# A recommender tower on one core: column sums as matmuls of 64 rows by 32 columns in two banks, and units 6 to 19 transposed by VectorE

## The chip, the cores and the metric

The kernel runs on one core of one Trainium2 chip. The metric is the device time of one execution in microseconds (us); three executions of the kernel before are given. The profile shows one execution of it, whose span begins at its first instruction and ends at its last.

## The reference

For 512 examples, 40 embedding rows of 64 numbers are looked up. Each of the 780 pairs of fields gets a bilinear score, and a three-layer network follows:

```python
e = jnp.stack([tbl_0[ids[:, 0]], ..., tbl_39[ids[:, 39]]], axis=1)   # 512 x 40 x 64
viW = jnp.einsum('bpd,pde->bpe', e[:, i_idx], W)                     # W: 780 x 64 x 64
z = jnp.einsum('bpe,bpe->bp', viW, e[:, j_idx])                      # 512 x 780
h = jnp.concatenate([z, dense_ctx], axis=1)                          # 512 x 796
h = jnp.maximum(h @ W_top1 + b_top1, 0.0)                            # 512
h = jnp.maximum(h @ W_top2 + b_top2, 0.0)                            # 256
y = h @ W_top3                                                       # 1
```

All of it is float32.

## The kernel before, in words

Two fields make a unit, so there are 20 units; `x[:, u, :]` holds unit u with its 128 numbers on the partitions and the 512 examples along the row. Units 0 to 3 come from small tables and are picked by matmuls with one-hot rows (L535). Units 4 to 19 are gathered: GpSimd issues eight indirect DMAs for each (L336; 2 fields by 4 chunks of 128 examples), in the order of the units, and they land with the examples on the partitions. So each has to be transposed. Units 4 to 10, 18 and 19 are transposed by TensorE (`transpose_unit`, L587) into the bank `t_ps` (unit 4 into `z_ps`) and copied out by ScalarE (`save_x`, L382). Units 11 to 17 (`FOLDED`) are transposed in squares of 32 by 32 by VectorE (`fold_unit`, L491), after which ScalarE puts the squares in place with 16 small copies (L389). GpSimd's first 24 gathers (units 4, 5 and 6) wait for no product; each later one waits for one product more than the gather before it.

The work on the pairs is cut in 195 **duos** in 49 **rounds** of four (three in the last). For a duo, TensorE multiplies two halves of `x` by weights, as two matmuls of 64 rows by 128 columns that run side by side (`interact`, L611), into one of three slots of `y_ps`. VectorE multiplies that slot by a factor out of `x` into `prod` (L522), the **product** of the duo. Duo d waits until product d - 3 has freed its slot. Two rounds later (`LAG`) TensorE sums `prod` over groups of partitions with a 0/1 matrix `select`: `sum_round` (L632), before the change in matmuls of 128 rows by 32 columns, four side by side, all into the bank `z_ps`. A round has eight of them. From round 25 on GpSimd first adds two products of a round into the other two (L352), and four are left. At every eighth round ScalarE copies `z_ps` out (`save_z`, L418).

A float32 matmul stands in the trace as two MATMUL records, and so does its weight load. A duo is thus 4 records on TensorE, the sums of a round 16 (8 from round 25 on), a transposed unit 4.

The order on each engine is the order in which the code is written: all engines walk the same list of duos. `transposed_at(u)` gives the duo ahead of which unit u is transposed, on TensorE (`transpose_unit`) or on VectorE (`fold_unit`) alike. Every engine works strictly through its own list, so an instruction that waits holds up all that stands behind it. After the last sums come layer 1 (L642), layer 2 (L682) and layer 3 (L691).

Of the kernel before, what the change touches and what calls it, by code (L numbers as in the profile page):

```python
# [12 lines left out]
ROWS = 128  # L13
BANK = 512
FIELDS = 40
DIM = 64
# [19 lines left out]
BLOCK_ROUNDS = QUAD // 4  # L36
# [3 lines left out]
FOLDED = range(11, 18)  # L40
# [24 lines left out]
class Plan:  # L65
# [7 lines left out]
    def __init__(self):  # L73
# [23 lines left out]
        self.blocks = -(-len(self.rounds) // BLOCK_ROUNDS)  # L97


        assert len(self.rounds) == BLOCK_ROUNDS * (self.blocks - 1) + 1 and ROUND * 4 + DENSE == QUAD  # L100
# [68 lines left out]
    def place(self, d, half):  # L169

        r, n = divmod(d, ROUND)
        row = 4 * (r % BLOCK_ROUNDS)
        if not self.is_quad(r):
            row += 2 * (n // 2)
        return r // BLOCK_ROUNDS, 2 * (n % 2) + half, row


def dlrm_tower(nc, ids, hot_ids, lane_rows, tables, w1_in, w2_in, head_in, dense_in, w_in, identity, selector, out):
# [6 lines left out]
    with ExitStack() as ctx:  # L185
# [11 lines left out]
        select = sb("select", [ROWS, 2, 2 * QUAD])  # L197
# [41 lines left out]
        h1_ps = [t_ps[:, :], y_ps[:, 0, 0, :], y_ps[:, 0, 1, :], y_ps[:, 1, 0, :]]  # L239

        h2_ps = [[y_ps[:, 1, 1, :], y_ps[:, 2, 0, :]], h1_ps[0:2]]
        out_ps = y_ps[:, 2, 1, 0:BATCH // 4]
# [113 lines left out]
        def _(act):  # L356
# [75 lines left out]
            if (len(plan.rounds) - LAG) // BLOCK_ROUNDS < NBLK - 1:  # L432
                save_z(NBLK - 2)
# [92 lines left out]
        def _(pe):  # L526
# [88 lines left out]
            def sum_round(r):  # L615

                b, _, row = plan.place(ROUND * r, 0)
                quad = plan.is_quad(r)
                if row == 0 and b:

                    pe.wait_ge(z_saved, b)
                closes = row == QUAD - 4 or r == len(plan.rounds) - 1
# [158 lines left out]
```

## Time and profile before

| | us |
|---|---|
| three executions | 357.65, 359.73, 360.52 (median 359.73) |
| span of the profiled execution | 320.2 |
| TensorE busy in the span | 312.7 |
| VectorE busy | 252.3 |
| GpSimd busy | 237.7 |
| ScalarE busy | 90.3 |

The profiled execution has no time of its own beside its span. Against the median of the three, 39.5 us lie around the span. Busy time counts an engine's overlapping instructions once.

### The profile page before, as it was taken

The page shows a single profiled execution, that of the slowest core. Times are in us where ns is not written, and L with a number is a line of the kernel's source. Part 1 is how long each engine was busy: PE and PEld are TensorE (multiplying, and loading weights), DVE is VectorE, ACT ScalarE, POOL GpSimd, SP SyncE. Part 2 cuts the span into 40 slices and gives each one's busy share as a digit, 9 for nine tenths or more (in the row PEclk, how much of TensorE's full clock was granted, in tenths as well). Part 3 has the DMA queues.
Part 4 walks back from the last instruction along what each step waited for, and adds up shares of the span by engine and source line. Part 5 has one row for each costly group of instructions (what it writes and reads, how often), then busy time and mean ns, then how long its engine had stood idle before and what let it go on. Part 6 is the DMA issues. An engine that isn't in the chain of part 4 may idle for free.

```text
span 320.2 us, 4340 instructions
## 1 busy us (share of the span) xinstructions
PE 312.7 (98%) x1716; PEld 117.5 (37%) x1716; DVE 252.3 (79%) x243; ACT 90.3 (28%) x206; POOL 237.7 (74%) x178
## 2 busy tenths in 40 slices
PE   6899999999999999999999999999999999989996
PEld 2465233332333323333333333333333333323464
DVE  4995987788689888988898899999999999940000
ACT  0203500600106835559976363000000000000032
POOL 3898777777777777776677999999999999940000
PEclk9999999999999999999999999999999999999999
DMA  6981332323323753232323121221121000000000
GB/s 136 358 243 21 82 72 62 92 59 67 87 57 92 253 171 86 61 93 57 88 60 90 41 66 34 66 68 46 52 68 57 0 2 0 0 3 5 12 0 0
DMA packets 14459, 23.27 MB, mean 73 GB/s; under 512 B 3556, under 2 KB 4584, under 8 KB 14312
## 3 DMA queue, kind: packets, MB, share of 16 engines
q1 hardware_dynamic: 7848, 13.96, 15.6%
q0 software_dynamic: 4096, 4.20, 6.4%
q10 hardware_dynamic: 2496, 4.84, 4.5%
q8 instruction: 13, 0.21, 0.3%
q14 instruction: 6, 0.05, 0.0%
HBM read 22.86 MB, written 0.00 MB: 71 GB/s over the span
## 4 chain that ended last, share of the span: by engine, by line
PE 65%; POOL 28%; DMA 3%; DVE 1%; POOLq 1%; ACT 0%; issue 0%; ACTq 0%
PE y_ps L611 33%; POOL prod L352 28%; PE z_ps L632 16%; PE y_ps L642 5%; PE y_ps L535 3%; DMA prod<-in_tbl 2%; PE t_ps L642 2%; PE y_ps L682 2%; PE t_ps L535 2%; PE t_ps L587 1%; DMA prod<-hot_ids 1%; DVE prod L522 1%; POOLq L185 1%; PE t_ps L682 1%; DVE x_quad L463 0%; PE y_ps L691 0%
## 5 line engine op out<-in xcount | busy, mean ns | idle before, releaser
L611 PE MATMUL y_ps<-x,w 64*128 64x512 f32 x780 | 183.3, 605 | 0.2
L336 POOL DMA_INDIRECT gathered<-in_tbl,ids_sb x128 | 130.6, 1020 | 45.7 <-issue 28.5
L522 DVE TENSOR_TENSOR prod<-y_ps,x 128x1024 f32<-128x1024 f32 x89 | 103.2, 1218 | 20.5 <-PE y_ps L611 20.1
L522 DVE TENSOR_TENSOR prod<-y_ps,x_quad 128x1024 f32<-128x1024 f32 x96 | 110.7, 1217 | 4.4 <-PE y_ps L611 3.7
L611 PEld LDWEIGHTS y_ps<-x,w 64*128 64x128 f32 x780 | 70.0, 186 | 108.3 <-issue 79.1
L352 POOL TENSOR_TENSOR prod<-prod 128x1024 f32<-128x1024 f32 x46 | 106.9, 2374 | 0.3
L632 PE MATMUL z_ps<-prod,select 128*32 128x512 f32 x596 | 74.5, 600 | 1.3 <-POOL prod L352 1.3
L389 ACT COPY x<-x_fold 32x128 f32<-32x128 f32 x112 | 33.1, 296 | 18.1 <-DVE x_fold L491 16.9
L632 PEld LDWEIGHTS z_ps<-prod,select 128*32 128x32 f32 x596 | 14.4, 108 | 54.1 <-issue 37.6
L418 ACT COPY zT<-z_ps 128x512 f32<-128x512 f32 x6 | 3.5, 586 | 100.6 <-PE z_ps L632 100.6
L412 ACT COPY x_mix<-x 64x512 f32<-64x512 f32 x40 | 24.7, 617 | 0.7
L382 ACT COPY x<-t_ps 128x512 f32<-128x512 f32 x8 | 4.7, 586 | 54.1 <-PE t_ps L587 54.1
L642 PE MATMUL y_ps<-zT,w 128*128 128x512 f32 (+1 forms) x42 | 17.0, 604 | 0.0
L399 ACT COPY x_quad<-x 32x512 f32<-32x512 f32 x24 | 14.8, 616 | 0.4
L522 DVE TENSOR_TENSOR prod<-y_ps,x_mix 128x1024 f32<-128x1024 f32 x10 | 11.8, 1217 | 1.9 <-issue 1.9
L642 PEld LDWEIGHTS y_ps<-zT,w 128*128 128x128 f32 (+1 forms) x42 | 7.0, 189 | 9.2 <-issue 9.2
L456 DVE TENSOR_SCALAR prod<-prod,lane_rows_sb 128x1024 bf16<-128x1024 int16 x16 | 6.9, 490 | 3.6 <-DMA lane_rows_sb<-lane_rows 3.2
L535 PE MATMUL y_ps<-prod 128*64 128x512 bf16 x32 | 6.7, 443 | 1.4 <-DVE x_quad L463 1.1
L642 PE MATMUL t_ps<-zT,w 128*128 128x512 f32 (+1 forms) x14 | 6.5, 606 | 0.0
L456 DVE TENSOR_SCALAR x<-prod,lane_rows_sb 128x1024 bf16<-128x1024 int16 x16 | 6.5, 477 | 0.0
L535 PE MATMUL y_ps<-prod,x_quad 128*64 128x512 bf16 x32 | 5.9, 381 | 0.6 <-DVE prod L456 0.6
L587 PEld LDWEIGHTS t_ps<-ident,gathered 128*128 128x128 f32 x32 | 3.4, 141 | 6.2 <-issue 6.2
(46 smaller groups left out, 87.5 us busy)
## 6 DMA issues: line engine op xcount, KB each, us to landing
w<-w_rows SPq DMA_DIRECT2D x48, 256.0 KB, 2.7
gathered<-in_tbl,ids_sb POOLq DMA_INDIRECT x128, 2.5
w<-w_rows ACTq DMA_DIRECT2D x1, 1792.0 KB, 8.0
prod<-in_tbl ACTq DMA_DIRECT2D x6, 256.0 KB, 8.5
prod<-hot_ids SPq DMA_DIRECT2D x4, 256.0 KB, 6.7
prod<-in_tbl ACTq DMA_DIRECT2D x4, 128.0 KB, 3.1
w<-w_rows ACTq DMA_DIRECT2D x1, 512.0 KB, 9.7
w<-w_rows SPq DMA_DIRECT2D x1, 192.0 KB, 2.3
```

Of the source, the lines that this page charges most:

```text
L336: nc.gpsimd.indirect_dma_start(gathered[:, slot, c, s * DIM:(s + 1) * DIM], None, tables[f][:, :], bass.IndirectOffsetOnAxis(ap=ids_sb[:, ...
L352: nc.gpsimd.tensor_tensor(prod[:, low, :, :], prod[:, low, :, :], prod[:, high, :, :], ALU.add).then_inc(added, 1)
L389: last = nc.scalar.copy(to[:, :, b * QUAD:(b + 1) * QUAD], x_fold[b * QUAD:(b + 1) * QUAD, u % 2, :, e * QUAD:(e + 1) * QUAD])
L399: last = nc.scalar.copy(x_quad[n * QUAD:(n + 1) * QUAD, u - PAIRED - u % 2 + h, :], x[s * DIM + h * QUAD:s * DIM + (h + 1) * QUAD, u, :])
L412: copied = nc.scalar.copy(x_mix[side * DIM:(side + 1) * DIM, 2 * n + half, :], x[field * DIM:(field + 1) * DIM, unit, :])
L456: nc.vector.tensor_scalar(hot[per_lane * u + q], hot_ids_sb[u], lane_rows_sb[:, q:q + 1], None, ALU.is_equal).then_inc(hot_ready, 1)
L522: nc.vector.tensor_tensor(prod[:, d % PROD_SLOTS, :, :], y_ps[:, d % DUO_SLOTS, :, :], factor, ALU.mult).then_inc(prod_ready, 1)
L535: last = nc.tensor.matmul(hot_ps[u][s * DIM:(s + 1) * DIM, :], weights, hot[per_lane * u + q][:, s * BATCH:(s + 1) * BATCH], start=q == 0 ...
L611: last = nc.tensor.matmul(y_ps[:, d % DUO_SLOTS, half, :], w[rows, r % W_SLOTS, d % ROUND, :], x[rows, units[half], :], start=True, stop=True)
L632: last = nc.tensor.matmul(z_ps[q * QUAD:(q + 1) * QUAD, :], select[:, 1 if quad else 0, QUAD - row:2 * QUAD - row], prod[:, d % PROD_SLOTS ...
L642: done = nc.tensor.matmul(h1_ps[m], w1[rows, b, m * ROWS:(m + 1) * ROWS], zT[rows, b, :], start=first and b == blocks[0], stop=last and b ...
L682: last = nc.tensor.matmul(h2_ps[n][m][:, batch_halves[n]], w2[:, k, m * ROWS:(m + 1) * ROWS], h1[k][:, batch_halves[n]], start=(k == 0), s ...
```

## The change

The sums are made of matmuls of 64 rows by 32 columns, upper and lower rows apart: the upper rows go into `z_ps`, the lower ones into `t_ps`. A round has 16 such matmuls in place of 8, and eight of them have places of their own in the array. A block takes 16 rounds and is then copied out of both banks. The duos' matmuls stay 64 rows by 128 columns. The last round, which has a block of its own, keeps matmuls of 128 rows.

`t_ps` is not free for transposes after the first sums, so only units 4 and 5 are transposed by TensorE, unit 5 ahead of duo 4 where it was ahead of duo 11. `FOLDED` is now units 6 to 19: seven more on VectorE, each with 16 copies of ScalarE in place of one. The rule for the place of a folded unit puts unit 6 ahead of duo 8, unit 7 ahead of duo 16, and so on by eights up to unit 19 ahead of duo 112. Before, units 6 to 10 stood ahead of duos 15, 21, 30, 38 and 46, and units 18 and 19 ahead of 104 and 112. The banks of the three layers are dealt out anew.

```diff
-BLOCK_ROUNDS = QUAD // 4
+BLOCK_ROUNDS = QUAD // 2
...
-FOLDED = range(11, 18)
+FOLDED = range(6, 20)
...
+        if u == HOT_UNITS + 1:
+
+            return ROUND
         if u >= FOLDED.start:
...
-            def save_z(b):
-                act.wait_ge(summed, BLOCK_ROUNDS * (b + 1))
-                nc.scalar.copy(zT[:, b, :], z_ps[:, :]).then_inc(z_saved, 1)
+            def save_z(block):
+                act.wait_ge(summed, BLOCK_ROUNDS * (block + 1))
+                for s in range(2):
+                    nc.scalar.copy(zT[:, 2 * block + s, :], z_halves[s][:, :]).then_inc(z_saved, 1)
...
                 for d in duos:
                     for half in range(2):
-                        _, q, row = plan.place(d, half)
-                        last = nc.tensor.matmul(z_ps[q * QUAD:(q + 1) * QUAD, :],
-                                                select[:, 1 if quad else 0, QUAD - row:2 * QUAD - row],
-                                                prod[:, d % PROD_SLOTS, half, :],
-                                                start=(r % BLOCK_ROUNDS == 0 and d < ROUND * r + 2),
-                                                stop=closes and d >= duos[-1] - 1)
+                        q = 2 * (d % 2) + half
+                        out = slice(q * QUAD, (q + 1) * QUAD)
...
+                        row = 2 * turn + (0 if quad else d % ROUND // 2)
+                        for s in range(2):
+                            rows = slice(s * DIM, (s + 1) * DIM)
+                            last = nc.tensor.matmul(z_halves[s][out, :],
+                                                    select[rows, 1 if quad else 0, QUAD - row:2 * QUAD - row],
+                                                    prod[rows, d % PROD_SLOTS, half, :],
+                                                    start=turn == 0 and d < ROUND * r + 2,
+                                                    stop=turn == BLOCK_ROUNDS - 1 and d >= duos[-1] - 1)
                 last.then_inc(summed, 1)
...
-            layer1(0, full[:-1], first=True)
+
+            pe.wait_ge(prod_ready, ROUND * (len(plan.rounds) - 1) + 1)
+            layer1(0, full[:-2], first=True)
             pe.wait_ge(z_saved, NBLK - 1)
-            layer1(0, full[-1:])
+            layer1(0, full[-2:])
```

VectorE at the start of the duos, before: the first products (5, 2 and 21 of them), with no transpose among the first 46.

```order
L522 TENSOR_TENSOR prod<-y_ps,x 128x1024 x5
L522 TENSOR_TENSOR prod<-y_ps,x_mix 128x1024 x2
L522 TENSOR_TENSOR prod<-y_ps,x 128x1024 x21
L522 TENSOR_TENSOR prod<-y_ps,x_mix 128x1024 x2
L522 TENSOR_TENSOR prod<-y_ps,x 128x1024 x18
L491 STREAM_TRANSPOSE x_fold<-gathered 128x512
```

VectorE at the same place now (L530 is the product, L499 the transpose of a folded unit):

```order
L530 TENSOR_TENSOR prod<-y_ps,x 128x1024 x5
L530 TENSOR_TENSOR prod<-y_ps,x_mix 128x1024 x2
L530 TENSOR_TENSOR prod<-y_ps,x 128x1024
L499 STREAM_TRANSPOSE x_fold<-gathered 128x512
L530 TENSOR_TENSOR prod<-y_ps,x 128x1024 x8
L499 STREAM_TRANSPOSE x_fold<-gathered 128x512
L530 TENSOR_TENSOR prod<-y_ps,x 128x1024 x8
```

The transpose of unit 6 stands behind eight products (duos 0 to 7) and ahead of that of duo 8; that of unit 7 follows eight products later.

TensorE from unit 4 to the second sums, before (two matmuls of L611 are a duo; L587 x4 is a transposed unit):

```order
L587 MATMUL z_ps<-ident,gathered 128x128 x4
L535 MATMUL t_ps<-x,zT 64x512 x16
L611 MATMUL y_ps<-x,w 128x512 x22
L587 MATMUL t_ps<-ident,gathered 128x128 x4
L611 MATMUL y_ps<-x,w 128x512 x2
L632 MATMUL z_ps<-prod,select 32x512 x8
L611 MATMUL y_ps<-x,w 128x512 x6
L587 MATMUL t_ps<-ident,gathered 128x128 x4
L611 MATMUL y_ps<-x,w 128x512 x2
L632 MATMUL z_ps<-prod,select 32x512 x8
```

TensorE at the same place now, down to the first four of the 16 sums of round 0 (L595 is the transpose, L619 the duos, L653 the sums):

```order
L595 MATMUL z_ps<-ident,gathered 128x128 x4
L543 MATMUL t_ps<-x,zT 64x512 x16
L619 MATMUL y_ps<-x,w 128x512 x8
L595 MATMUL t_ps<-ident,gathered 128x128 x4
L619 MATMUL y_ps<-x,w 128x512 x16
L653 MATMUL z_ps<-prod,select 32x512
L653 MATMUL t_ps<-prod,select 32x512
L653 MATMUL z_ps<-prod,select 32x512
L653 MATMUL t_ps<-prod,select 32x512
```

Unit 5's transpose moves from behind 11 duos to behind four, the transposes of units 6 to 10, 18 and 19 are gone from TensorE, and the sums alternate between the two banks.

## Rows read from the trace of the kernel before

**Rows 1.** The page: TensorE's busy time, and the chain that ended last.

```profile
PE 312.7 (98%) x1716; PEld 117.5 (37%) x1716; DVE 252.3 (79%) x243; ACT 90.3 (28%) x206; POOL 237.7 (74%) x178
...
PE 65%; POOL 28%; DMA 3%; DVE 1%; POOLq 1%; ACT 0%; issue 0%; ACTq 0%
```

**Rows 2.** Busy us (count) by stretch: PE, PEld, DVE, ACT, POOL; clock, DMA.

```profile
44.90:175.60 130.70, 130.70 (x764) 45.08 (x760) 110.96 (x99) 62.29 (x160) 96.98 (x103) 1.00 0.35 92
175.60:279.00 103.40, 103.40 (x543) 36.24 (x542) 100.40 (x88) 12.36 (x21) 102.96 (x46) 1.00 0.14 39
```

**Rows 3.** Chain that ended last, rounds of duos: start us, us, what.

```profile
92.01 1.92 PE y_ps L611 x8
93.92 0.59 PE t_ps L587 x4
...
147.68 3.63 PE y_ps L611 x16
151.31 1.85 PE z_ps L632 x16
153.16 3.63 PE y_ps L611 x16
156.80 1.85 PE z_ps L632 x16
...
184.83 0.99 PE z_ps L632 x8
185.82 0.59 PE t_ps L587 x4
```

**Rows 4.** The same chain in the tail: sums between layer 1's matmuls of 128x128.

```profile
285.11 5.35 PE t_ps L642 x12
290.46 1.84 PE z_ps L632 x12
292.30 10.50 PE y_ps L642 x24
```

**Rows 5.** The sums' weight loads: four in the timeline, and the page's mean (ns).

```profile
152.13 0.13 PEld L632 LDWEIGHTS z_ps<-prod,select 128*32 128x32 f32 x4 [0.30 <-issue]
```

```profile
L632 PEld LDWEIGHTS z_ps<-prod,select 128*32 128x32 f32 x596 | 14.4, 108 | 54.1 <-issue 37.6
```

**Rows 6.** Timeline of VectorE: a round's products, then a folded unit.

```profile
148.78 4.62 DVE L522 TENSOR_TENSOR prod<-y_ps,x 128x1024 f32<-128x1024 f32 x4 [0.87 <-PE y_ps L611]
153.32 0.70 DVE L491 STREAM_TRANSPOSE x_fold<-gathered 128x512 f32<-128x512 f32 x1
```

**Rows 7.** Timeline of ScalarE: the copies of one folded unit.

```profile
98.70 4.90 ACT L389 COPY x<-x_fold 32x128 f32<-32x128 f32 x16 [3.56 <-DVE x_fold L491]
```

**Rows 8.** Gathers: POOL busy and count to 44.6 us, the last of them, time to landing.

```profile
0.00:44.60 44.60, 32.38 (x24) 1.00 0.57 157
```

```profile
43.45 0.94 POOL L336 DMA_INDIRECT gathered<-in_tbl,ids_sb  x1 [0.30 <-issue]
```

```profile
DMA to landing us min/median/max: 2.3/2.5/7.5
```

**Rows 9.** Timeline of VectorE (duos 7 to 11) and TensorE (duo 11, round 3).

```profile
39.05 5.74 DVE L522 TENSOR_TENSOR prod<-y_ps,x 128x1024 f32<-128x1024 f32 x5
```

```profile
41.97 1.13 PE L611 MATMUL y_ps<-x,w 64*128 64x512 f32 x4
...
44.88 1.56 PE L611 MATMUL y_ps<-x,w 64*128 64x512 f32 x6
```

**Rows 10.** The same chain: GpSimd's additions.

```profile
191.09 90.58 POOL prod L352 x39
```

**Rows 11.** TensorE: early and later one-hot matmuls; a stretch behind its last matmul (clock 0.71).

```profile
5.39 1.92 PE L535 MATMUL y_ps<-prod 128*64 128x512 bf16 x8 [0.34 <-DMA prod<-in_tbl]
...
28.03 1.92 PE L535 MATMUL t_ps<-x,zT 128*64 128x512 bf16 x16
```

```profile
320.00:323.00 3.00, 0.00 (x0) 0.00 (x0) 0.00 (x0) 0.00 (x0) 0.00 (x0) 0.71 0.03 5
```

More of the change, by code:

```diff
@@ L96, in __init__ @@
         self.duos = [d for r in self.rounds for d in r]
-        self.blocks = -(-len(self.rounds) // BLOCK_ROUNDS)
-        assert len(self.rounds) == BLOCK_ROUNDS * (self.blocks - 1) + 1 and ROUND * 4 + DENSE == QUAD
+        self.turns = len(self.rounds) // BLOCK_ROUNDS
+        self.blocks = 2 * self.turns + 1
+        assert len(self.rounds) == BLOCK_ROUNDS * self.turns + 1 and ROUND * 4 + DENSE == QUAD
         self.gather_after = self.gather_times()
@@ L167, in mixture, with place @@
         }[kind]
-    def place(self, d, half):
+    def place(self, d, half, side):
         r, n = divmod(d, ROUND)
[L172 to L175, printed above, removed]
+        q = 2 * (n % 2) + half
+        if r == len(self.rounds) - 1:
+            return self.blocks - 1, q, 2 * (n // 2) + side
+        block, turn = divmod(r, BLOCK_ROUNDS)
+        if self.is_quad(r):
+            return 2 * block + side // 2, q, 2 * turn + side % 2
+        return 2 * block + side, q, 2 * turn + n // 2
 def dlrm_tower(nc, ids, hot_ids, lane_rows, tables, w1_in, w2_in, head_in, dense_in, w_in, identity, selector, out):
@@ L431, in _ @@
                     save_z((r - LAG) // BLOCK_ROUNDS)
-            if (len(plan.rounds) - LAG) // BLOCK_ROUNDS < NBLK - 1:
-                save_z(NBLK - 2)
+            for block in range((len(plan.rounds) - LAG) // BLOCK_ROUNDS, plan.turns):
+                save_z(block)
             act.wait_ge(summed, len(plan.rounds))
@@ L615, in sum_round @@
             def sum_round(r):
-                b, _, row = plan.place(ROUND * r, 0)
+                block, turn = divmod(r, BLOCK_ROUNDS)
                 quad = plan.is_quad(r)
-                if row == 0 and b:
-                    pe.wait_ge(z_saved, b)
-                closes = row == QUAD - 4 or r == len(plan.rounds) - 1
+                if r == 0:
+                    pe.wait_ge(x_ready, HOT_UNITS + 2)
+                elif turn == 0:
+                    pe.wait_ge(z_saved, 2 * block)
                 if r in plan.added:
@@ L711 @@
     identity = np.eye(ROWS, dtype=np.float32)
-    selector = np.zeros((ROWS, 2, 2 * QUAD), np.float32)
+    selector = np.zeros((ROWS, 3, 2 * QUAD), np.float32)
     for e in range(ROWS):
-        selector[e, 0, QUAD + e // DIM] = 1.0
-        selector[e, 1, QUAD + e // QUAD] = 1.0
+        selector[e, 0, QUAD] = 1.0
+        selector[e, 1, QUAD + e % DIM // QUAD] = 1.0
+        selector[e, 2, QUAD + e // DIM] = 1.0
     W = np.asarray(inputs["L0_rec_W"])
@@ L724 @@
         for half in range(2):
-            b, q, row = plan.place(d, half)
             for side, pair in enumerate(plan.tile_pairs(d, half)):
@@ L730 @@
                 w_rows[half * DIM:(half + 1) * DIM, d, side * n:(side + 1) * n] = (W[p] if i < j else W[p].T)[:, part]
+                b, q, row = plan.place(d, half, side)
                 if b < plan.blocks - 1:
-                    w1_rows[q * QUAD + row + side, b] = W_top1[p]
+                    w1_rows[q * QUAD + row, b] = W_top1[p]
                 else:
                     for m, columns in parts:
-                        w1_rows[m * QUAD + ROUND * q + row + side, b, columns] = W_top1[p, columns]
+                        w1_rows[m * QUAD + ROUND * q + row, b, columns] = W_top1[p, columns]
     pairs = FIELDS * (FIELDS - 1) // 2
```

15 lines of the change are left out of this document (11 added, 4 removed).

## The prediction

> **What bounds the kernel now.** I read the page's chain first [rows 1]: TensorE 65% of the span, GpSimd 28%. TensorE is busy 98% of the time, but that is a mean over stages, so I cut the span [rows 2]. From 44.9 to 175.6 us (rounds 3 to 25) TensorE has no idle time, VectorE has 15%: here every us on TensorE counts and a little more on VectorE costs nothing. From 175.6 to 279 TensorE, VectorE (97%) and GpSimd are all full. GpSimd's additions follow each other every 90.58 / 39 = 2.32 us, 4.65 a round [rows 10]; TensorE's round is 3.63 + 0.99 = 4.62 [rows 3]; VectorE's products come one per 1.12 (five in 5.74, four in 4.62), four in 4.5 [rows 6, 9]. What TensorE saves there is worth nothing. Ahead of 44.9 VectorE sets the pace of the first duos, product behind product [rows 9].
>
> **The sums.** A plain round is 3.63 of duos and 1.85 of sums, 5.48 together, with a folded unit inside it or not: the starts 147.68, 153.16 and 151.31, 156.80 both lie 5.49 apart, and the fold at 153.32 is in the second only [rows 3, 6]. What is in these blocks? In the tail 12 steps of 512 columns take 5.35 and 24 take 10.50 [rows 4], so a step is 5.15 / 12 = 0.429 and a block loses 0.20 on entry. The eight steps of four duos are 3.43, and 3.63 stand there: again 0.20. The sums' 16 records, four at a time, are four steps, 1.72, and 1.85 stand there: 0.13. So the two switches of a round cost 0.33. Afterwards the sums have 32 records, eight at a time: again four steps. The work of the array is the same, and only the 0.33 could shrink. Does it? The two shapes now have the same 64 rows and differ in columns alone. The trace has such a case: the last sums (128x32) stand between layer 1's matmuls (128x128), rows equal, columns not. Their four steps take 1.84, a loss of 0.12, and the block behind them loses 0.20 [rows 4]. That is what switches of rows and columns together cost. I take nothing off.
>
> [...]
>
> There is a small loss instead. Four weight loads of 108 ns each are over in 0.13, so one begins some 7 ns behind the other [rows 5]. With eight places the last begins four times 7 = 0.027 later, and the switch waits for it. In 23 rounds on TensorE's path that is **+0.6**. In the last stage TensorE's round becomes 4.65, level with GpSimd's: **+0.2** for some 20 rounds. Bounds: 0 and 1.2.
>
> **The transposes that leave TensorE.** Units 6 to 10 stand in the middle of a round: 0.59, and the duos are then 1.92 + 1.92 where 3.63 would do [rows 3], 0.80 each. Five make **-4.0**. Unit 18 stands beside a sum block: **-0.6**. Unit 19 (0.59 at 185.82, [rows 3]) lies in the stage in which all three engines are full. Its fold takes 0.70 of VectorE [rows 6], which has 0.1 to spare per round, so 0.6 comes back: **0**. The folds of units 7 to 18 hide in VectorE's 0.87 of idle time per round [rows 6]; if that were gone, 0.7 each.
>
> ScalarE now spends 4.9 us per folded unit where one copy did [rows 7], every second round (11 us). It is under half busy in the pair stage [rows 2]. The tightest unit is 7: folded ahead of duo 16, needed as factor of duo 21, five duos or 6.9 us later, against 0.7 + 4.9. That holds with 1.2 to spare; what is beyond it would be paid once. The copies out of the sums' banks are two in a row now, but only three times, and a whole block of duos (3.6 us) stands ahead of the sums that wait for them. In the tail only banks change hands.
>
> **The gathers.** This is the term that decides. Unit 6 is now folded ahead of duo 8. VectorE's wait for its gathers holds up every later product, and through the three slots TensorE too. Gathers up to unit 6 are 24, and they don't depend on products: GpSimd issues them as fast as it can, one per 1.25 us, and the 24th starts at 43.45 [rows 8]. It lands 2.5 later, say at 46.1 (46.0 to 46.5). The product of duo 8 starts at 39.05 + 1.12 = 40.17 before [rows 9]. So VectorE stands for nearly six us. Before, unit 6 stood ahead of duo 15 and waited for nothing. Step by step: landing 46.1, fold 0.70, product of duo 8 1.25, then wait and weight load some 0.2, and the matmuls of duo 11 start at 48.25. Before they started at 41.97 [rows 9], and from there on both kernels do the same up to round 3. **+6.3.** Unit 5, now ahead of duo 4, meets the same limit (16th gather, ten us earlier, landing near 36), but what it delays is over before 46.1 and costs nothing more. Later units are safe: their gathers come at 10 us per unit, their folds every two rounds, 11 us.
>
> **The sum.** 6.3 - 4.0 - 0.6 + 0 + 0.6 + 0.2 = **+2.5**: a span of 322.7 for 320.2, and with the 39.5 around it 362.2 beside the median of 359.73. Between the bounds of the terms (gathers 6.1 to 6.8, start-up of the sums 0 to 1.2, unit 19 -0.6 to +0.2, unit 7 up to 1) it is 360.8 to 363.8.
>
> **Rivals.** (1) *The clock falls in the hole*, the case on the slower side. Duo 10's matmuls are done near 44.1 (product 7 ends near 42.9, since duo 4 was held to about 37, and one duo takes 1.2), and duo 11's begin at 48.25: over four us without a matmul, where from round 3 on there was no hole at all [rows 2]. [...] At the start the same shape gave 8 records in 1.92 where it later gave 16 [rows 11]: half pace. A fall costs half of the time spent low: at least 1.0 (those 1.92), at most 3.0, if it lasts six us. It decides if the hole is long enough; the time is 363.2 to 365.2, I take 364.3. Against it: no hole of that size inside a trace shows what happens. 0.33.
>
> [...]
>
> (2) *The switches get cheaper after all*, since both shapes split the rows alike. At best the 0.33 goes, but in every second round VectorE with four products and a fold (5.2) caps it at 0.3; the last stage gains nothing. 23 x 0.3 = 6.9, and no 0.6 of staggering: 354.7. For it: no case in the trace has 64 rows on both sides. Against it: the tail's switch. 0.11.
>
> (3) *The change doesn't do what it says*: the eight don't run side by side but four by four. 596 / 8 = 74 groups of two steps would take 0.86 more each, over 420. Against it: two 64-row matmuls already write the same partitions of two banks side by side, and four columns of 128 rows run together. 0.05.
>
> **How the numbers follow.** My forecast has 0.48, the rivals 0.33, 0.11 and 0.05, and 0.03 is left. A measurement of this kernel can tell about 1%, 3.6 us. Faster by more (below 356.1): rival 2, 0.11. Slower by more (above 363.3): rival 3, nearly all of rival 1 and the upper end of the forecast, 0.42. Within: 0.47. The range goes from 357.0, half of rival 2's gain, to 366.5, past rival 1; outside lie rival 3 and most of rival 2.
>
> **What would show it.** VectorE idle for about 5 us ahead of the first transpose of a folded unit, released by a gather, and TensorE idle to 48.2; the granted clock behind it tells rival 1. Round 3 starts 6.3 later, at 51.2. Plain rounds of 5.49 to 5.52, sum blocks of 1.88 or so in four steps, no 0.59 between them. Round 26 starts near 178. Additions every 2.32. If sum blocks are near 1.7 or duo blocks near 3.45, rival 2 holds. I am wrong if the gathers of unit 6 land much before 46, or if the rounds differ from 5.5 by more than 0.1.

## The result, and the profile after

| | median of executions, us | ratio to the kernel before |
|---|---|---|
| before | 358.69 (357.1 to 360.52, 4) | |
| changed | 376.14 (375.49 to 377.02, 4) | 1.057 [1.049, 1.065] |

The medians lie 17.5 us apart, 4.9% of the kernel before. The recorded ratio, 1.057, is taken over fast executions alone, and can't be worked out from the times shown. The prediction was 362.2, and the range of 357.0 to 366.5 doesn't reach the measured time. The profiled execution of the changed kernel has a time of its own: 377.02, with a span of 375.1. So 1.9 us lie around this span, not 39.5. It suggests that the profile of before, with its span of 320.2, came from an execution unlike those that were timed, and e0 below shows it.

The page of the changed kernel, the rows that answer to [rows 1], with the granted clock and two of the costliest groups:

```profile
span 375.1 us, 5562 instructions
...
PE 322.3 (86%) x2272; PEld 116.4 (31%) x2272; DVE 256.7 (68%) x250; ACT 118.9 (32%) x311; POOL 238.6 (64%) x178
...
PEclk9899866999999999999999989999999999999999
...
PE 44%; POOL 36%; DVE 8%; issue 6%; another core or an unknown queue 3%; DMA 2%; POOLq 1%; ACT 0%; ACTq 0%; DVEq 0%
...
L619 PE MATMUL y_ps<-x,w 64*128 64x512 f32 x780 | 193.1, 622 | 42.5 <-DVE prod L530 36.6
L343 POOL DMA_INDIRECT gathered<-in_tbl,ids_sb x128 | 131.5, 1027 | 99.9 <-DVE prod L530 63.8
```

TensorE's share fell from 98% to 86%, GpSimd's from 74% to 64%, VectorE's from 79% to 68%. No engine is full: all of them wait. The windows of the changed kernel, cut at the first duo, round 3, round 26 and round 48 (columns as in [rows 2]):

```profile
30.48:63.56 33.08, 18.34 (x86) 6.34 (x85) 13.96 (x13) 11.41 (x27) 20.97 (x23) 0.74 0.20 47
63.56:230.01 166.45, 135.46 (x1113) 43.62 (x1105) 113.60 (x104) 77.70 (x218) 86.97 (x93) 0.99 0.26 69
230.01:334.00 103.99, 103.78 (x729) 36.18 (x721) 101.86 (x91) 20.40 (x50) 103.71 (x46) 1.00 0.14 40
```

The stage of additions takes 103.99, next to 103.40 in [rows 2]. The pair rounds 3 to 25 take 166.45 where they took some 131, with 135.46 of TensorE's work in them: 31 us are waits. The stretch ahead of round 3 takes 33.08, and it took 15.00 (29.88 to 44.88); its granted clock is 0.74, and in windows of one us it reads 0.50 from 39 to 42 and from 50 to 62 us.

One pair round in the timeline of the changed kernel, VectorE, TensorE's duos, then GpSimd:

```profile
117.85 3.47 DVE L530 TENSOR_TENSOR prod<-y_ps,x 128x1024 f32<-128x1024 f32 x3
123.99 4.62 DVE L530 TENSOR_TENSOR prod<-y_ps,x 128x1024 f32<-128x1024 f32 x4 [2.67 <-PE y_ps L619]
...
117.99 1.13 PE L619 MATMUL y_ps<-x,w 64*128 64x512 f32 x4 [1.48 <-DVE prod L530]
120.93 2.85 PE L619 MATMUL y_ps<-x,w 64*128 64x512 f32 x12
125.27 1.13 PE L619 MATMUL y_ps<-x,w 64*128 64x512 f32 x4 [1.50 <-DVE prod L530]
...
120.70 0.95 POOL L343 DMA_INDIRECT gathered<-in_tbl,ids_sb  x1 [0.30 <-issue]
121.95 0.94 POOL L343 DMA_INDIRECT gathered<-in_tbl,ids_sb  x1 [0.30 <-issue]
125.49 0.94 POOL L343 DMA_INDIRECT gathered<-in_tbl,ids_sb  x1 [2.59 <-DVE prod L530]
```

TensorE begins the first duo of round 11 at 120.93. In [rows 6] VectorE starts its product some 1.2 us behind a round's first matmul (147.61 and 148.78). Here it starts at 123.99, 3.06 behind, and gives TensorE as the reason. But by then TensorE has run all three duos for which there are slots (120.93 + 2.85 = 123.78), and waits in turn for that product. The ring is closed: TensorE waits for VectorE, VectorE for a signal of TensorE, GpSimd for VectorE. Each turn takes 7.28 us.

The semaphores' updates in the trace show where it breaks. The sums of this round end at 121.00, and the signal that they are done arrives at 123.91. The signals of duos 0, 1 and 2, due at 122.06, 122.92 and 123.77, all arrive at 123.97 to 124.09. VectorE's and ScalarE's own signals, those that the trace holds, come within 0.02 us of their instructions' ends. So from 121.00 to 123.91 no signal of TensorE got through, though its matmuls were issued on time; then four came 0.06 apart. In each of the rounds 3 to 21 the sums' signal is 2.8 to 3.2 us late, and it comes 0.95 to 1.12 us behind the end of the last gather of a row of three or four (here 122.90 and 123.91). The ends of matmuls are modelled by the profile, so it can't tell a signal that lags behind its matmul from a matmul that itself ends late; "late signal" stands for both. In the stage of additions, where no gathers run, the sums' signals are 0.08 late.

**One word for what follows.** I call an execution *prompt* if TensorE's signals in the pair rounds come within 0.3 us of the matmuls' ends, and *late* if not. The profile of before is prompt: 0.04 to 0.05 us.

### The profile page after: what moved, and what is told of

Read it like the earlier page. It is cut to its first block, busy times and chain, and to the rows that moved or that the text cites. A ratio compares the mean times of both kernels' runs of the same rounds, so it can differ in the third digit from the quotient of the medians.

```text
span 375.1 us, 5562 instructions
## 1 busy us (share of the span) xinstructions
PE 322.3 (86%) x2272; PEld 116.4 (31%) x2272; DVE 256.7 (68%) x250; ACT 118.9 (32%) x311; POOL 238.6 (64%) x178
## 3 DMA queue, kind: packets, MB, share of 16 engines
q0 software_dynamic: 4096, 4.20, 5.6%
q10 hardware_dynamic: 2496, 4.87, 3.8%
## 4 chain that ended last, share of the span: by engine, by line
PE 44%; POOL 36%; DVE 8%; issue 6%; another core or an unknown queue 3%; DMA 2%; POOLq 1%; ACT 0%; ACTq 0%; DVEq 0%
POOL prod L359 28%; PE y_ps L619 23%; PE z_ps L653 12%; POOL gathered L343 8%; DVE prod L530 8%; PE y_ps L663 6%; PE y_ps L705 2%; DMA ids_sb<-ids_rows 1%; PE t_ps L653 1%; POOLq L191 1%; DMA gathered<-in_tbl,ids_sb 1%; DVE x_fold L499 1%; PE z_ps L646 0%; PE t_ps L714 0%
## 5 line engine op out<-in xcount | busy, mean ns | idle before, releaser
L619 PE MATMUL y_ps<-x,w 64*128 64x512 f32 x780 | 193.1, 622 | 42.5 <-DVE prod L530 36.6
L530 DVE TENSOR_TENSOR prod<-y_ps,x 128x1024 f32<-128x1024 f32 x89 | 103.3, 1218 | 62.9 <-PE y_ps L619 45.8
L619 PEld LDWEIGHTS y_ps<-x,w 64*128 64x128 f32 x780 | 70.5, 189 | 163.0 <-issue 93.1
L530 DVE TENSOR_TENSOR prod<-y_ps,x_quad 128x1024 f32<-128x1024 f32 x96 | 110.7, 1217 | 8.3 <-PE y_ps L619 4.1
L396 ACT COPY x<-x_fold 32x128 f32<-32x128 f32 x224 | 66.2, 295 | 101.6 <-issue 79.3
L653 PE MATMUL z_ps<-prod,select 64*32 64x512 f32 x584 | 75.0, 609 | 1.1 <-POOL prod L359 1.1
L653 PE MATMUL t_ps<-prod,select 64*32 64x512 f32 x584 | 75.0, 609 | 0.0
L653 PEld LDWEIGHTS z_ps<-prod,select 64*32 64x32 f32 x584 | 16.0, 108 | 54.1 <-issue 46.9
L663 PE MATMUL y_ps<-zT,w 128*128 128x512 f32 (+1 forms) x56 | 22.4, 604 | 0.0
L530 DVE TENSOR_TENSOR prod<-y_ps,x_mix 128x1024 f32<-128x1024 f32 x10 | 11.9, 1219 | 6.1 <-issue 5.5
L653 PEld LDWEIGHTS t_ps<-prod,select 64*32 64x32 f32 x584 | 16.0, 108 | 0.0
L499 DVE STREAM_TRANSPOSE x_fold<-gathered 128x512 f32<-128x512 f32 x14 | 9.8, 701 | 0.0
L705 PE MATMUL y_ps<-prod,w 128*128 128x256 f32 x32 | 7.3, 382 | 0.0
L450 ACT ACTIVATE prod<-y_ps,head 128x512 f32<-128x512 f32 x4 | 2.5, 685 | 14.5 <-PE y_ps L663 14.5
```

The costliest lines, as they stand in the source:

```text
L396: last = nc.scalar.copy(to[:, :, b * QUAD:(b + 1) * QUAD], x_fold[b * QUAD:(b + 1) * QUAD, u % 2, :, e * QUAD:(e + 1) * QUAD])
L499: nc.vector.transpose(x_fold[:, u % 2, :, :], gathered[:, u % GATHER_SLOTS, :, :]).then_inc(unit_folded, 1)
L530: nc.vector.tensor_tensor(prod[:, d % PROD_SLOTS, :, :], y_ps[:, d % DUO_SLOTS, :, :], factor, ALU.mult).then_inc(prod_ready, 1)
L619: last = nc.tensor.matmul(y_ps[:, d % DUO_SLOTS, half, :], w[rows, r % W_SLOTS, d % ROUND, :], x[rows, units[half], :], start=True, stop=True)
L653: last = nc.tensor.matmul(z_halves[s][out, :], select[rows, 1 if quad else 0, QUAD - row:2 * QUAD - row], prod[rows, d % PROD_SLOTS, half, :],
L663: done = nc.tensor.matmul(h1_ps[m], w1[rows, b, m * ROWS:(m + 1) * ROWS], zT[rows, b, :], start=first and b == blocks[0], stop=last and b ...
```

## The experiments

**The theories.** A: the profile of before shows an unusual execution, and its usual ones have late signals as well. S: the form of the new sums (64 rows, eight side by side) delays the signals. N: their number does. G: GpSimd's indirect gathers, issued one behind another, hold them back. C, after the second group: whether signals are late at all is a condition of a group of runs, and without it the change costs what its steps add up to.

They ran in six groups, each with executions of the kernel before beside it:

| group | kernel before, us (executions) | kind |
|---|---|---|
| 1: e0 to e3 | 359.18, 354.30 to 364.19 (19) | late |
| 2: e4 to e7 | 322.89, 321.38 to 327.85 (13) | prompt |
| 3: e8 to e10 | 357.75, 354.54 to 359.52 (13) | late |
| 4: e11 to e14 | 324.03, 321.79 to 327.68 (25) | prompt |
| 5: e15, e16 | 324.33, 321.46 to 328.14 (19) | prompt |
| 6: e17 | 323.38, 322.19 to 326.83 (13) | prompt |

No execution of the kernel before lies between 328.2 and 354.2. The kind holds through a group. The chips are numbered, and number 2 stands with group 1 and with group 4, so the number doesn't decide it. The three timings given with the profile (357.65 to 360.52) are of the late kind, the profile is of the prompt kind.

**e0, the kernel before, unaltered.**

> The kernel before, once more, for its spans. The profile shown of it spans 320.2 us, its executions take 357 to 360. Theory A (the profile shown is one fast execution, the usual one is slower inside): the span is near 356 and plain rounds take about 1.4 us more than 5.49. Theory B (39 us lie around the span of this kernel): the span is 320 again, rounds 5.49, sums signalled 0.04 us behind the end of their last matmul.

Measured: 360.75 (356.93 to 362.94, ten executions), ratio 1.0011 [0.9954, 1.0068], span of the profiled one 360.9. The same cuts, and three rounds in its timeline, VectorE and TensorE (L611 duos, L632 sums, L587 a transposed unit):

```profile
30.18:62.70 32.52, 19.48 (x70) 5.85 (x68) 13.67 (x12) 6.69 (x11) 21.39 (x24) 0.74 0.16 40
62.70:216.27 153.57, 136.95 (x765) 44.49 (x761) 111.59 (x100) 62.30 (x160) 86.91 (x93) 0.98 0.27 77
...
109.73 4.62 DVE L522 TENSOR_TENSOR prod<-y_ps,x 128x1024 f32<-128x1024 f32 x4 [0.75 <-issue]
117.41 4.62 DVE L522 TENSOR_TENSOR prod<-y_ps,x 128x1024 f32<-128x1024 f32 x4 [3.05 <-PE y_ps L611]
...
108.56 3.70 PE L611 MATMUL y_ps<-x,w 64*128 64x512 f32 x16
112.19 1.92 PE L632 MATMUL z_ps<-prod,select 128*32 128x512 f32 x16
114.05 1.99 PE L611 MATMUL y_ps<-x,w 64*128 64x512 f32 x8
118.69 1.13 PE L611 MATMUL y_ps<-x,w 64*128 64x512 f32 x4 [1.01 <-DVE prod L522]
```

The kernel before has late signals too, but in every second round only. Of the rounds that begin at 108.56 and 114.05 the first runs through in 5.49, and in the second the product waits 3.05. The sums' signals of the rounds around them are late by 0.05, 3.21, 0.04 and 3.33 us. Two rounds take 13.04 us (108.56 to 121.60), where two of the changed kernel take 14.56. The change meets the lateness twice as often. The 15 us ahead of round 3 are 32.5 in this kernel as well, with a granted clock of 0.74 here too.

**e1, the folds alone.** The kernel before with the two lines that move the transposes:

```diff
-FOLDED = range(11, 18)
+FOLDED = range(6, 20)
...
+        if u == HOT_UNITS + 1:
+            return ROUND
```

> The kernel before with units 6 to 19 folded on VectorE and unit 5 transposed ahead of duo 4; the sums stay 128 rows by 32 columns in one bank. Theory S (the long pair rounds of the changed kernel, 7.28 us, come from the eight-wide sums, whose signal comes 2.9 us behind their last matmul): plain rounds as in the kernel before, the hole ahead of duo 8 and the lower clock stay, time some 12 to 15 us over the same kernel without the hole's loss, about 10 over before. Theory F (they come from the folds and ScalarE's 16 copies): rounds of 7.3 us, time near 376.

Measured: 363.38 (358.09 to 369.28, ten executions), ratio 1.0039 [0.9985, 1.0093]. The pair stage of its trace takes 150.29 us. The larger part of the loss comes from the sums.

**e2, unit 6 folded later.**

```diff
         if u >= FOLDED.start:
+            if u == FOLDED.start:
+                return 12
```

> The changed kernel with unit 6 folded ahead of duo 12, not 8: VectorE has four more products to do until the gathers of unit 6 land. If the hole with its lower clock costs what the profile of the changed kernel shows (round 3 begins at 63.6 us, 18.7 later than before), 8 to 14 us are saved and the clock stays up. If the hole is only moved, 0 to 3 us.

Measured: 376.65, ratio 1.0466 [1.0383, 1.0548], the time of the changed kernel. Round 3 begins at 63.13, where it began at 63.56. So to fold unit 6 later gives next to nothing back; that VectorE stands in this stretch in any case would explain it, but isn't shown apart.

**e3, the sums in another order.** The 16 matmuls of a block: the eight of the upper rows, then the eight of the lower rows. It was meant to have four places in use at a time.

```diff
+                turns = [(d, half, s) for s in range(2) for d in duos for half in range(2)]
```

> The changed kernel with the 16 matmuls of a round's sums in another order: the eight of the upper rows, then the eight of the lower ones. Only four places of the array are then used at a time. If the eight matmuls side by side cause the late signal (theory W, width), the signal comes at most 0.1 us behind the last matmul, the sum block grows from 1.95 to about 3.6 us and rounds of 7.2 us are bound by TensorE. If the number of 64-row matmuls causes it (theory N), the signal is 2.9 us late as before and the round takes 8 us or more.

Measured: 377.34, ratio 1.0486 [1.0407, 1.0564], pair stage 166.0 us as before. But the edit didn't narrow the block. Its first two steps in the timeline, upper rows (`z_ps`) and lower rows (`t_ps`):

```profile
126.47 0.63 PE L646 MATMUL z_ps<-prod,select 64*32 64x512 f32 x4
126.53 0.63 PE L646 MATMUL t_ps<-prod,select 64*32 64x512 f32 x4
126.93 0.61 PE L646 MATMUL z_ps<-prod,select 64*32 64x512 f32 x4
126.98 0.61 PE L646 MATMUL t_ps<-prod,select 64*32 64x512 f32 x4
```

Upper and lower rows still run side by side, and the block takes 1.97 us (126.47 to 128.44) and not the 3.6 that was expected. So the run shows that the order of the sixteen makes no difference. Whether the eight side by side delay the signals it doesn't tell; their number, their 64 rows and their being eight wide all stay possible.

**e4, plain copies for gathers.** In the changed kernel, for every gather after the 24th, a copy of the table's first 128 rows (the lookup is left out):

```diff
+                if g - first >= GATHERED_FIRST:
+                    nc.gpsimd.dma_start(gathered[:, slot, c, s * DIM:(s + 1) * DIM],
+                                        tables[f][0:ROWS, :]).then_inc(unit_gathered[slot], 16)
+                    return
```

> The changed kernel, except that GpSimd's queue fetches each half unit after the first 24 with a plain copy of the first 128 rows of the table, in place of the indirect gather: the same bytes, queue, waits and semaphores, no lookup (the left-out lookup makes the outputs those of other rows). Theory G (GpSimd's indirect gathers, issued one after another, are what holds TensorE's signals back): the signals of the pair rounds come within 0.1 us of the matmuls' ends, a round takes 5.5 us in place of 7.28, and the time falls by 20 x 1.8 = some 30 to 36 us, to 340 to 346. Theory N (the number of matmuls in a row holds them back): 7.28 us a round and 374 to 378 as before.

Measured: 326.79, ratio 1.0137 [1.0045, 1.0228]. The group was prompt, so it told nothing of the lateness (its repeat e9 does). What showed was the size of the other thing: 323 against 359 for the same kernel before.

**e5, more matmuls in the kernel before.**

```diff
+                        if not starts and not quad:
+                            nc.tensor.matmul(z_ps[q * QUAD:(q + 1) * QUAD, 0:16], select[:, 0, 0:QUAD],
+                                             prod[:, d % PROD_SLOTS, half, 0:16], start=False, stop=False)
```

> The kernel before, with one small matmul more (zero weights, 16 columns, it adds nothing) ahead of each of the eight sums' matmuls of a pair round: nearly no work, but as many matmuls and weight loads in a round as in the changed kernel (96 records for 64). Theory N: signals are late in every pair round, not in every second one, rounds near 7.3 us and a time of 370 to 378. Theory S (64-row matmuls, eight at a time, are what is special) and theory G: 359 plus the small matmuls' own 16 x 0.01 to 0.06 a round, 360 to 366, with late signals in every second round.

Measured, prompt: 327.63, ratio 1.0207 [1.0093, 1.0321]; the sums' signals 0.06 us late. A pair round takes 5.65 for 5.49, so eight small matmuls (16 records) cost 0.16 us a round.

**e6, half of the sums.** The changed kernel without the sums of two of a round's four duos (`duos = duos[:2]`).

> The changed kernel without the sums of the third and fourth duo of each pair round (left out; those rows of z stay zero): 8 matmuls of 64 x 32, still eight at a time, 64 records a round. TensorE loses 0.86 us of work a round. Theory N: signals late in every second round at most, a round 4.7 to 6.6 us, time 330 to 362. Theory S: signals 2.9 us late after every block, the loop of 7.28 us stays or shrinks by the 0.86 alone: 6.4 to 7.3 us a round, 355 to 376.

Measured, prompt: 320.93, ratio 0.9937 [0.9894, 0.998], though TensorE loses two steps of 0.429 us ([rows 4]), 0.86 together, in some 23 rounds. The pair stage shrinks from 126.77 (e14) to 112.11 us, 0.64 a round, but the stage of additions grows from 103.58 to 108.92 and the rest from 41.43 to 45.32. At its end GpSimd is still behind with gathers: its first addition begins at 174.29, where the matmuls of round 25 began at 161.22. One gather per 1.25 us is 5.0 a round, more than the 4.87 that the round now takes. So sums made cheaper by more than some 0.5 us a round meet GpSimd next; the 0.3 of rival 2 (a round of 5.2) would not have reached that.

**e7, the sums in two blocks,** eight matmuls behind duo 1 and eight behind duo 3.

```diff
+                    if r > LAG and d == ROUND * r + 1 and r - LAG not in plan.added:
+                        sum_round(r - LAG, 0)
```

> The changed kernel with the sums of a pair round in two blocks of eight matmuls, one behind duo 1 and one behind duo 3 (the same matmuls, two switches more, 0.3 us a round). If a block of 16 matmuls in a row is what makes the signals late (theory N by block): signals within 0.1 us, rounds of 5.8 us, time 345 to 355. If it is the number of matmuls in a round, or the gathers alone: signals still late, rounds of 7 to 7.6 us, time 372 to 382.

Measured, prompt: 333.67, ratio 1.0345 [1.0257, 1.0434]. The chain of waits in one round, where each line is from one kind of matmul to the next (rows of 0.01 left out):

```profile
111.13 1.92 PE y_ps L619 x8
113.05 0.54 PE z_ps L655
...
113.64 0.38 PE z_ps L655
...
114.07 1.92 PE y_ps L619 x8
```

A half round is 2.94, a round 5.88, where the unsplit one takes 5.51. The matmuls are the same. One more pair of switches costs 0.37 us. The prediction's estimates come to 0.36: 0.33 and a second stagger of 0.03.

**e8, the changed kernel, unaltered.**

> The changed kernel, unaltered. The four kernels before it ran on another chip, where the kernel before takes 322.9 us and not 359, with rounds of 5.49 us and signals within 0.1 us of the matmuls' ends. Theory C (the late signals belong to some chips; what the change itself costs is what its own steps add up to): where the kernel before takes some 323 us, this one has rounds of 5.51 us and takes 325 to 331; where the kernel before takes some 359 us, it has rounds of 7.28 us and takes 375 to 378. Theory S (the new sums delay the signals wherever they run): 7.28 us a round and 355 to 365 us beside 323.

Measured, late: 372.96 (372.72 to 373.1), ratio 1.042 [1.0346, 1.0493]. Both theories allow this one; e14 tells them apart.

**e9, plain copies again,** the kernel of e4, now in a late group.

> The changed kernel with plain copies in place of the gathers after the first 24 (the lookup of those units is left out), as run before. On a chip where the kernel before takes 323 us: 325 to 329 again. On one where it takes 359 us this is the test that is still open. Theory G (indirect gathers in a row hold TensorE's signals back there): 5.5 us a round and 338 to 346. Against theory G: 7.28 us a round and 374 to 378.

Measured: 327.67 (326.85 to 329.09), 45.3 us under the changed kernel of the same group, ratio to before 0.9147 [0.9082, 0.9212]. Its pair stage in the windows, and its groups of GpSimd's copies and gathers:

```profile
55.54:182.57 127.03, 127.03 (x1112) 44.82 (x1105) 112.72 (x103) 77.76 (x218) 48.86 (x91) 1.00 0.30 90
...
L344 POOL DMA_DIRECT2D gathered<-in_tbl x104 | 55.9, 540 | 82.8 <-DVE prod L534 82.6 <-issue 0.2
L347 POOL DMA_INDIRECT gathered<-in_tbl,ids_sb x24 | 32.3, 1344 | 11.7 <-issue 7.0 <-DMA ids_sb<-ids_rows 4.7
```

TensorE has no idle time in the pair stage, the sums' signals are 0.08 to 0.09 late in every round, and a round takes 5.51. Ahead of the pair rounds, while and just after the 24 indirect gathers that this kernel keeps are issued, its own signals are late: a duo's matmuls end at 41.23, the signal comes at 46.84, 5.6 us later, and VectorE waits for it:

```profile
46.93 1.22 DVE L534 TENSOR_TENSOR prod<-y_ps,x 128x1024 f32<-128x1024 f32 x1 [2.31 <-PE y_ps L623]
```

So this very execution has the condition of its group, and loses the lateness where its gathers stop. Theory G is right that the lateness needs the gathers: 104 of them turned into plain copies, with nothing else in the program changed, take it away. It had the size wrong (338 to 346). I had counted 20 rounds of 1.8; against e8 the pair stage gives 38.4 us (165.41 and 127.03), and the stretch ahead of it another 5.7 (30.78 and 25.07). What of a gather does it is open. A plain copy holds GpSimd for 0.54 us where a gather holds it 1.0, in the pair rounds it leaves gaps of 0.6 us and more between two where gathers leave 0.3, and it reads neighbouring rows of the table.

The queue q0 carries 4096 packets and 4.20 MB in both kernels (e8 and e9). So it isn't the queue or the bytes.

**e10, the folds alone again,** late.

> The kernel before with the transposes of units 6 to 19 by VectorE and unit 5 ahead of duo 4, sums as before, as run already beside 359 us (ratio 1.004). On a chip where the kernel before takes 323 us: by the steps of the prediction the gathers' hole costs 6.3 and the transposes give 4.6 back, plus 1 to 2 for TensorE's clock: 324 to 328, the same as the changed kernel within 1.5 us. On one with 359 us: 360 to 366.

Measured: 358.87, ratio 1.0064 [1.0019, 1.0109]. Its pair stage:

```profile
60.30:210.02 149.72, 132.28 (x737) 43.27 (x737) 114.81 (x105) 77.83 (x218) 88.30 (x94) 0.98 0.29 78
```

149.72 beside 153.57 of e0 and 165.41 of e8. The new sums cost 15.7 us there. The folds save 3.9 by e0 and e10, which are of two groups, and 3.3 by e0 and e1, which are of one. Its signals are late in every second round, as in e0.

**e11, the kernel before with plain copies.**

> The kernel before with plain copies in place of the gathers after the first 24 (the lookup of those units is left out). Theory G: no late signals in the pair rounds, 5.49 us a round, on a chip where the kernel before takes 355 to 360 us too: 318 to 325, some 4 us under the 327.7 of the changed kernel with plain copies, which is then what the change costs by itself. Against theory G: 355 to 360.

Measured, prompt: 323.72, ratio 0.9969 [0.9915, 1.0023]. Where signals are prompt, gathers cost the kernel nothing.

**e12, every second gather a plain copy** (`and g % 2` in the condition of e4).

> The changed kernel with every second gather after the first 24 a plain copy (52 of 104; the lookup of those parts is left out). On a chip with late signals, if each gather holds signals back for a time of its own: late by a part of the 2.8 us, 6.0 to 6.8 us a round, 340 to 362. If only gathers that follow one another without a gap do it: signals on time, 5.51 us a round, 328 to 333. On a chip without late signals: 326 to 331.

Measured, prompt: 327.94, ratio 1.0111 [1.0026, 1.0196]. Its question is about late groups and stays open.

**e13, more matmuls again.**

> The kernel before with one small matmul more ahead of each sums' matmul of a pair round (as run before on a chip without late signals, where it took 327.6 beside 322.9). On a chip with late signals. Theory N (more matmuls, more lateness): late in every pair round, near 7.3 us a round, 370 to 378. Against it: late in every second round, 358 to 366.

Measured, prompt once more: 326.70, ratio 1.0121 [1.0067, 1.0175].

**e14, the changed kernel, unaltered.**

> The changed kernel, unaltered, for the case that the call falls on a chip where the kernel before takes some 323 us: by the prediction's own terms 325 to 331 there, rounds of 5.51 us. If it falls on a chip with 355 to 360: 372 to 378 as before.

Measured, prompt: 328.41 (325.47 to 331.7, ten executions), ratio 1.0112 [1.0066, 1.0158], span of the profiled one 325.3. That settles theory C against theory S: the new sums delay no signal by themselves. The windows with the same cuts, then two windows of six us that show the clock, then a round in the timeline (VectorE, TensorE's duos, GpSimd):

```profile
30.34:53.57 23.23, 16.92 (x86) 6.05 (x85) 14.72 (x13) 11.41 (x27) 17.44 (x20) 0.85 0.25 61
53.57:180.34 126.77, 126.77 (x1112) 44.69 (x1104) 112.74 (x103) 77.75 (x218) 90.69 (x97) 1.00 0.34 92
180.34:283.92 103.58, 103.50 (x728) 36.32 (x720) 101.75 (x91) 20.41 (x50) 103.28 (x46) 1.00 0.14 40
...
36.00:42.00 6.00, 4.47 (x14) 2.08 (x16) 1.93 (x3) 1.25 (x3) 4.61 (x5) 0.72 0.17 44
48.00:54.00 6.00, 4.86 (x38) 1.38 (x40) 4.56 (x4) 4.73 (x16) 4.48 (x6) 0.72 0.28 72
...
120.89 4.62 DVE L530 TENSOR_TENSOR prod<-y_ps,x 128x1024 f32<-128x1024 f32 x4 [0.84 <-PE y_ps L619]
...
119.71 3.71 PE L619 MATMUL y_ps<-x,w 64*128 64x512 f32 x16
...
120.67 0.94 POOL L343 DMA_INDIRECT gathered<-in_tbl,ids_sb  x1 [0.30 <-issue]
122.38 0.94 POOL L343 DMA_INDIRECT gathered<-in_tbl,ids_sb  x1 [0.76 <-DVE prod L530]
```

The round begins at 119.71 and its first product at 120.89, 1.18 behind, as in [rows 6]. GpSimd's gathers follow one another here with the same 0.3 between them as in the late executions.

**e15, every second gather again, and e16 and e17, more matmuls twice more.**

> The changed kernel with every second gather after the first 24 a plain copy (the lookup of those parts is left out); it took 327.9 beside 324.0 on a chip without late signals. On a chip with late signals (the kernel before 355 to 360 us): if each gather holds signals back for a time of its own, 6.0 to 6.8 us a round, 340 to 362; if only gathers that follow one another without a gap do it, signals on time, 5.51 us a round, 328 to 333.

> The kernel before with one small matmul more ahead of each sums' matmul of a pair round; it took 327 beside 323 to 324 on two chips without late signals. On a chip with late signals (the kernel before 355 to 360 us). Theory N (more matmuls, more lateness): late in every pair round, near 7.3 us a round, 370 to 378. Against it (the form of the sums, or their place in time, decides): late in every second round, 358 to 366.

> The kernel before with one small matmul more ahead of each sums' matmul of a pair round, once more, since the question is only answered where signals are late (the kernel before at 355 to 360 us). Theory N (more matmuls, more lateness): late in every pair round, near 7.3 us a round, 370 to 378. Against it: late in every second round, 358 to 366. Where the kernel before takes 323: 326 to 329, and the question stays open.

Measured, all prompt: 326.47, ratio 1.0071 [1.0022, 1.0121]; 328.11, ratio 1.0093 [1.0031, 1.0155]; 325.75, ratio 1.0065 [1.0018, 1.0112]. I had hoped for a late group and got none. They say again that more matmuls cost about 1% where signals are prompt (0.7 to 2.1% over the four runs), and nothing on lateness.

## Why the prediction was wrong

**The step that failed** is the base, "a span of 322.7 for 320.2, and with the 39.5 around it 362.2". I took 39.5 us for a fixed cost around the span and worked out the change in the rhythm of the profile. Around a span lie 1.9 us (up to 3.6 in single executions). The other 37 to 38 are lost inside it, where signals of TensorE come late while gathers run, and the profile shows none of it. In e0, beside that profile, the stretch ahead of round 3 is 17.5 us longer (32.52 and 15.00), in part because TensorE is granted 0.74 of its clock there (0.50 from 42 to 51 and from 56 to 62 us), and the pair stage 22.8 (153.57 and 130.76). In the pair stage the changed kernel waits for late signals in every round, the kernel before in every second: 15.7 us more (e8 against e10). None of my rivals had this, since nothing in the profile had it.

The difference between 320.2 and 359.73 was in front of me, and I called it what lies around the span. I had no execution whose time and span were both known, so I could not know what lies around one. I should have made a rival of it: that the timed executions hold 37 us of waits which the profile doesn't show.

**The terms of the sum** were worked out for prompt executions and can be judged there. The profile of before against e14, stage by stage:

| stage | before | e14 | difference | predicted |
|---|---|---|---|---|
| start to first duo | 29.88 | 30.34 | +0.5 | 0 |
| first duo to round 3 | 15.00 | 23.23 | +8.2 | +6.3, or +8.4 with rival 1 |
| round 3 to round 26 | 130.76 | 126.77 | -4.0 | -4.0 -0.6 +0.6 = -4.0 |
| round 26 to round 48 | 103.30 | 103.58 | +0.3 | +0.2 |
| round 48 to the end | 41.25 | 41.42 | +0.2 | 0 |

Over ten executions and more, the difference of prompt medians is 4.4 us (328.41 and 324.03), and the recorded ratio, 1.0112, makes it 3.6 (2.1 to 5.1). I had predicted 2.5, and 4.6 with rival 1. (The bounds of my terms add up to 360.6 to 364.3, where I wrote 360.8 to 363.8; nothing hangs on it.)

- *Gathers, +6.3: the mechanism was right, its size too small.* VectorE in e14, answering to [rows 9]:

```profile
34.99 1.22 DVE L530 TENSOR_TENSOR prod<-y_ps,x 128x1024 f32<-128x1024 f32 x1
39.73 1.23 DVE L530 TENSOR_TENSOR prod<-y_ps,x 128x1024 f32<-128x1024 f32 x1 [3.52 <-PE y_ps L619]
...
43.92 1.22 DVE L530 TENSOR_TENSOR prod<-y_ps,x 128x1024 f32<-128x1024 f32 x1
47.27 0.71 DVE L499 STREAM_TRANSPOSE x_fold<-gathered 128x512 f32<-128x512 f32 x1 [2.13 <-DMA gathered<-in_tbl,ids_sb]
```

The fold begins at 47.27, released by a gather, where I said 46.1. The 24th gather starts at 44.63 and not at 43.45, and its landing takes the 2.6 that I had allowed. Counted from the first duo that gather is 0.7 later than in the profile of before. Ahead of this hole there is another, 3.52 us ahead of the product at 39.73: unit 5, now ahead of duo 4, for whose gathers TensorE stands 3.49 us. I had written that it "costs nothing more". It costs no product, but see the clock. It also kept the later hole of TensorE short: duo 10's matmuls end at 46.3, not near 44.1, and duo 11's begin at 49.14, 2.83 without a matmul where I had said over four.

- *Rival 1 came true.* The granted clock is 0.72 in both six-us windows. In windows of one us it reads 0.50 from 39 to 42, behind unit 5's hole, and from 49 to 52, behind unit 6's; with their edges each of the two lasts some 3.4 us, where I had allowed up to six. Duo 11's four records take 2.08 us in the second (at 49.14), where four take 1.13 in [rows 9], so close to half of the time spent low is lost, as I had it. What makes the clock fall, and how long a hole has to be for it, no run shows. Of the 8.2 us, 6.7 are there when duo 11 begins (18.80 behind the first duo, 12.09 before): the predicted 6.3, and 0.4 for the later gather. The other 1.5 come from there to round 3 (4.43 and 2.91), where the clock is low, between the 1.0 and 3.0 that I gave. In the late executions the hole doesn't stand out: the stretch takes 30.3 to 35.9 us with the folds (after, e1, e2, e3, e8, e10), and 32.52 (e0) without them.
- *Transposes, -4.0 and -0.6, and the stagger, +0.6: right in their sum.* 126.77 against 130.76. Under late signals the folds give 3.3 (e0 and e1) or 3.9 (e0 and e10).
- *The sums, no gain: right.* Four steps, eight matmuls side by side, rounds of 5.51 against the 5.49 of [rows 3]; rival 3 is out. The round less twelve steps of 0.429 leaves 0.36 for the two switches and the stagger, by the estimates 0.33 and 0.03, and e7 measured one more pair at 0.37; rival 2 is out.
- *The last stage, +0.2: right,* 0.3.
- What I had named as the sign of being wrong, "if the rounds differ from 5.5 by more than 0.1", is what happened: 7.28.

**What stays open.** Why a group is late or prompt: the kernels are the same. One thing does differ ahead of the first late signal, and that is how complete the traces are. Of 32 updates that VectorE makes of one semaphore ahead of the first duo, the trace of the changed kernel and the seven of late groups, e9 among them, hold 19 to 23, and the twelve prompt ones 31 or 32. Of updates by DMAs the former hold 1364 to 1677 (e9: 2950), the latter 3156 to 3316. This may be a second sign of the same cause; or the recording takes part in holding the signals back. Every execution of the six groups was recorded with its span, so no run tells the two apart. What in an indirect gather holds the signals back is open too: its 1.0 us on GpSimd, the short gaps, or the rows that it reads. And why the changed kernel meets this in every round: e1 and e10 put it on the new sums, and leave their number (96 records in a round for 64), their 64 rows, or their being eight side by side. The four runs that would have told (e5, e13, e16, e17) all fell in prompt groups. A late signal of 2.9 us also keeps GpSimd from its next gathers for 2.6, so each round hands the next the same start. That may be why the pattern is so regular, but it is argued, not shown.

## What to carry to other kernels

Set the profile's span beside the timed executions before working out any change. Here 1.9 us (up to 3.6) lay around a span whose own time is known, and 39.5 between the span of before and the timed executions. Where so much is left over and you don't have the profiled execution's own time, the profile may show another rhythm than the one that is timed, and a sum made on it is off by whatever the change does to the waits that it lacks. When an engine waits for a producer that seems long done, look at when the semaphore was updated and not at the instruction's modelled end. The ring of three engines with three slots had no room here for a signal that is 3 us late: a round took 7.28 us (the changed kernel's first run) where it took 5.51 (e14). And a change that hardly lengthened any engine's work in it (prompt rounds of 5.51 for 5.49) doubled how often it was hit.

## What the runs showed of the hardware

- TensorE's signals can arrive about 3 us behind the matmuls' modelled ends (2.8 to 3.2 in the changed kernel's rounds 3 to 21; 5.6 once in e9, ahead of round 3), in bunches 0.06 apart, while the recorded ones of VectorE and ScalarE come within 0.02. Seen only while indirect gathers run or just behind them, in two of six groups of runs and in the first run of the changed kernel, and by their times in the executions of before given at the start; there it cost the kernel before some 35 us of 359 and the changed one some 45 of 373. With the same number of plain copies the sums' signals came 0.08 to 0.09 late.
- The same kernel on the same kind of chip takes 323 or 358 us, by group, and nothing between.
- A switch between matmuls of 64 x 128 and 64 x 32, there and back, costs 0.37 us (e7), though both have 64 rows; a matmul of 16 columns and 128 x 32 costs 0.02 us (0.16 for eight, e5).
- In e14 the granted clock read 0.50 from 39 to 42 and from 49 to 52 us (0.72 over 36 to 42 and over 48 to 54). TensorE had stood for 3.49 us up to 37.53 and for 2.83 us up to 49.14, and was busy for 4.5 and 4.9 us of the two longer windows. Four records of a duo took 2.08 us at 49.14, and 1.13 in [rows 9].
- Late executions, and e9 in a late group, lack records in their traces: 9 to 13 of 32 updates by VectorE ahead of the first duo, where the prompt ones lack one at most.
